# Row maxima of attention in the sampling taps: from single matmuls to pairs of heads

## What is computed

```
x = x + attention(gn(x))
    q, k, v = split(tokens @ w_qkv.T)
    attn = softmax(q @ k.T * SCALE) ; out = (attn @ v) @ w_proj.T + b_proj
x = x + gelu(batch_norm(deform_conv(gn(x))))
    offset = clip(conv(x, off_w)) ; mask = 2 * sigmoid(conv(x, mask_w))
    p = bilinear samples of x at tap + offset, times mask ; y = einsum(p, w)
```

## Time and profile before

| | |
|---|---|
| median of 3 runs | 3905.09 us (3904.13 to 3913.32) |
| profiled execution | 3908.9 us, its span 3907.0 us |
| mean granted TensorE clock | 0.959 of 2.4 GHz |
| TensorE busy | 3494.0 us (89%), 33434 matmuls |
| VectorE busy | 2220.8 us (57%) |
| ScalarE busy | 1628.7 us (42%) |
| GpSimd busy | 1216.0 us (31%) |

### The profile page before, as it was taken

How to read it: one execution, slowest core, us unless ns; L and a number is a source line. 1 busy time by engine, 2 the same in 40 slices (tenths; PEclk the granted TensorE clock), 3 DMA queues, 4 the chain that set the end, 5 groups by cost and what they waited for, 6 DMA issues and landing times.

```text
span 3907.0 us, 88793 instructions
## 1 busy us (share of the span) xinstructions
PE 3494.0 (89%) x33434; PEld 1884.3 (48%) x33434; DVE 2220.8 (57%) x3746; ACT 1628.7 (42%) x2644; POOL 1216.0 (31%) x1182
## 2 busy tenths in 40 slices
PE   5788999989999899898998899998999989998992
PEld 2244554545445454454544454454544545454661
DVE  5565565655655566555665556565565555655343
ACT  3054333633335434453335433363333633344443
POOL 0042232612325123332324233262232512333440
PEclk8689999999999999999998999999999999999896
DMA  3000000000000000000000000000000000001007
GB/s 125 1 18 34 1 1 35 3 33 1 1 35 2 33 1 2 36 34 1 1 2 36 34 1 1 23 15 33 1 1 35 2 33 1 1 19 66 1 1 291
DMA packets 12152, 97.81 MB, mean 25 GB/s; under 512 B 2777, under 2 KB 2905, under 8 KB 4972
## 3 DMA queue, kind: packets, MB, share of 16 engines
q1 hardware_dynamic: 9468, 67.41, 4.5%
q0 software_dynamic: 1152, 12.58, 0.8%
q10 hardware_dynamic: 1008, 11.01, 0.7%
HBM read 56.26 MB, written 34.60 MB: 23 GB/s over the span
## 4 chain that ended last, share of the span: by engine, by line
PE 53%; issue 24%; POOL 13%; ACT 4%; DVE 3%; DMA 1%; POOLq 0%; DVEq 0%; SPq 0%; ACTq 0%
PE R L1492 20%; PE R L1473 13%; POOL PL L607 12%; PE G L1270 7%; PE G L1237 5%; PE G L1461 2%; PE R L1385 2%; ACT PL L830 1%; PE G L1453 1%; PE R L1310 1%; PE G L1412 1%; ACT P L769 1%; PE G L1407 1%; DMA QK<-x_scratch 1%; DVE M L1166 0%
## 5 line engine op out<-in xcount | busy, mean ns | idle before, releaser
L1492 PE MATMUL R<-P,WALL 128*128 128x512 f16 x3888 | 984.8, 380 | 0.3 <-issue 0.3
L989 DVE TENSOR_REDUCE MXP<-G 128x1 f32<-128x512 f32 x1024 | 698.5, 689 | 257.6 <-PE G L1270 243.6
L607 POOL TENSOR_TENSOR PL<-P 128x1024 f16<-128x1024 f32 x256 | 515.7, 2017 | 760.2 <-ACT P L752 760.2
L1473 PE MATMUL R<-MHL,XB 128*128 128x240 f16 (+14 forms) x7776 | 726.3, 236 | 2.5 <-DVE P L1187 2.5
L644 POOL TENSOR_TENSOR MHL<-M,MHL 128x280 f16<-128x280 f32 (+2 forms) x576 | 364.6, 635 | 995.7 <-ACT MHL L840 994.5
L752 ACT ACTIVATE P<-R 128x1024 f32<-128x1024 f32 x512 | 521.0, 1023 | 306.1 <-PE R L1310 305.9
L1473 PEld LDWEIGHTS R<-MHL,XB 128*128 128x128 f16 x7776 | 536.3, 98 | 154.7 <-issue 108.6
L1492 PEld LDWEIGHTS R<-P,WALL 128*128 128x128 f16 x3888 | 345.3, 98 | 416.5 <-issue 95.6
L1039 DVE TENSOR_TENSOR PL<-P 128x1024 f16<-128x1024 f32 x256 | 366.0, 1430 | 292.0 <-ACT P L752 291.9
L1310 PE MATMUL R<-QK 48*128 48x512 f16 (+1 forms) x3072 | 444.0, 397 | 52.4 <-issue 32.3
L1270 PE MATMUL G<-QK 48*128 48x512 f16 x1024 | 412.6, 404 | 44.3 <-DVE QK L977 17.5
(11 more groups left out here) (125 smaller groups left out, 3235.1 us busy)
## 6 DMA issues: line engine op xcount, KB each, us to landing
XA<-x SPq DMA_DIRECT2D x8, 1536.0 KB, 8.9
X<-x SPq DMA_DIRECT2D x8, 1536.0 KB, 6.6
x_scratch<-X SPq DMA_DIRECT2D x7, 1536.0 KB, 5.1
y_scratch<-XP ACTq DMA_DIRECT2D x7, 1536.0 KB, 6.8
WALL<-y_scratch SPq DMA_DIRECT2D x6, 1536.0 KB, 15.1
out<-WALL POOLq DMA_DIRECT2D x6, 1536.0 KB, 10.9
QK<-x_scratch SPq DMA_DIRECT2D x4, 1536.0 KB, 17.6
P<-wd SPq DMA_DIRECT2D x9, 576.0 KB, 4.8
```

The lines of the kernel that those rows point to most:

```text
L607: pool.tensor_tensor(PL[:, s % P_BUFS, :], P32[:, s % P_BUFS, :], high_view(s), ALU.subtract).then_inc(p_low_pool, 1)
L989: dve.reduce_max(MXP[:, name[1] % 2, n // 2, n % 2:n % 2 + 1], chunk(sec, name)[:, :], AX.X).then_inc(dve_read, 1)
L1473: last = pe.matmul(out, XT[:, x_part, g * BOX_Y + r, t * 128:(t + 1) * 128], MHL[:, m_part, o + at:o + at + (hi - lo) * (x1 - x0)], start= ...
L1492: last = pe.matmul(R6[:, CT + ct, :], WALL[:, w:w + 128], PHL[:, u % 2, part // 2, t, :], start=(u % TAPS == 0 and n < CT), stop=(u % TAPS ...
```

## The change

The order of the maxima changes: for each tile and key half, head 0 and then head 1 (MAXIMA). In the samples they stand in columns 1 and 3, two in each, and none in 0 and 2. In the convolutions the second of a pair stands at the same spot as the first. Unit 0 has one pair, in column 3; units 1 to 5 have two pairs in the samples and one in the convolutions; units 6 to 17 two and two. `pos` stays at 2; `mask` stands where its place in the list puts it. The maxima before batch 0 keep their order (ALL_MAXIMA). Every matmul and every reduction is as it was, in form and number.

```
-MAXIMA = [("max", i, n) for i in range(PAIRS) for n in range(4 * QT)]
+MAXIMA = [("max", i, hd * 2 * QT + n) for i in range(PAIRS) for n in range(2 * QT) for hd in range(2)]
+ALL_MAXIMA = [("max", i, n) for i in range(PAIRS) for n in range(4 * QT)]
...
-    convs[0] = made[:3]
-    made = made[3:]
+    convs[0], made = made[:3], made[3:]
     due = []
-    for u in range(1, UNITS):
-        samples[u], maxima = maxima[:4], maxima[4:]
-        convs[u], due = due, []
-        convs[u] += made[:2]
-        made = made[2:]
-        count = 2 if u < 5 else 4
+    for u in range(UNITS):
+        first = 1 if u == 0 else 2
+        samples[u], maxima = [[]] * (4 - 2 * first) + sum(([[], maxima[2 * k:2 * k + 2]] for k in range(first)), []), \
+            maxima[2 * first:]
+        convs[u] += due
+        count = 0 if u == 0 else 2 if u < 6 else 4
+        convs[u] += made[:2] if u > 0 else []
+        made = made[2:] if u > 0 else made
         convs[u] += maxima[:count]
         maxima = maxima[count:]
...
-    return [("pos", u + 2)] + fills[:1] + [("mask", u + 2)] + fills[1:]
+    at = 2 if fills and fills[0][0] == "max" else 1
+    return [("pos", u + 2)] + fills[:at] + [("mask", u + 2)] + fills[at:]
...
-def spots(n):
-
-    return ([2, 6] + [13 + 13 * k // max(1, n - 2) for k in range(n - 2)])[:n]
+def spots(names):
+
+    out = []
+    for k, name in enumerate(names):
+        if name[0] == "max" and k and names[k - 1][0] == "max" and name[2] == names[k - 1][2] + 2 * QT:
+            out.append(out[-1])
+        elif name[0] == "pos":
+            out.append(2)
+        elif k == 1 and name[0] != "max":
+            out.append(6)
+        else:
+            out.append(13 + 13 * max(0, k - 1) // max(2, len(names) - 1))
+    return out
...
                             sample(u, c, 0, 0)
                             if not final and c < len(SAMPLE_FILL[u]):
-                                fill_chunk(SAMPLE_FILL[u][c], sec, b + 1)
+                                for name in SAMPLE_FILL[u][c]:
+                                    fill_chunk(name, sec, b + 1)
                             sample(u, c, 1, 0)
```

More of the change, by code:

```diff
@@ L128, in slot_fills @@
     samples, convs, maxima, made = [[] for _ in range(UNITS)], [[] for _ in range(UNITS)], list(MAXIMA), list(QK[5:])
-    convs[0] = made[:3]
-    made = made[3:]
+    convs[0], made = made[:3], made[3:]
     due = []
-    for u in range(1, UNITS):
-        samples[u], maxima = maxima[:4], maxima[4:]
-        convs[u], due = due, []
-        convs[u] += made[:2]
-        made = made[2:]
-        count = 2 if u < 5 else 4
+    for u in range(UNITS):
[6 more added lines that the diff above has]
+        made = made[2:] if u > 0 else made
         convs[u] += maxima[:count]
         maxima = maxima[count:]
-        due = [("maxT", n[1]) for n in samples[u] + convs[u] if n[0] == "max" and n[2] == 4 * QT - 1]
+        due = [("maxT", n[1]) for n in sum(samples[u], []) + convs[u] if n[0] == "max" and n[2] == 4 * QT - 1]
     if maxima or made or due != [("maxT", PAIRS - 1)]:
@@ L177, in start_chunks @@
         for k in range(4):
-            out += MAXIMA[(4 * i + k) * QT:(4 * i + k + 1) * QT]
+            out += ALL_MAXIMA[(4 * i + k) * QT:(4 * i + k + 1) * QT]
             if i + 1 < PAIRS:
@@ L205, in tap_chunks @@
             if start and c < len(SAMPLE_FILL[u]):
-                out += with_readers([SAMPLE_FILL[u][c]])
+                out += with_readers(SAMPLE_FILL[u][c])
             nu, nc = ahead(u, c, reach)
@@ L1178, in taps @@
                             if not final and c < len(SAMPLE_FILL[u]):
-                                read_chunk(SAMPLE_FILL[u][c], sec, b + 1)
+                                for name in SAMPLE_FILL[u][c]:
+                                    read_chunk(name, sec, b + 1)
                             nu, nc = ahead(u, c, reach)
@@ L1528, in taps @@
                         done = 0
-                        for name, end in zip(names, spots(len(names))):
+                        for name, end in zip(names, spots(names)):
                             if u > 0:
```

## The result

The changed kernel takes 3932.37 us (median of 6 runs, 3922.14 to 3941.38), the kernel before 3909.27 in the same comparison: a ratio of 1.0057, 95% interval 1.0038 to 1.0075. **It is slower by about 23 us**, where no change was forecast, with 3882 to 3930 as the range. The profiled execution took 3925.8 us against 3908.9.

What follows compares the result with a forecast made beforehand. TensorE was taken to set the pace of the taps, with VectorE mattering by when it gives a bank back. Unit gains and waits summed to 0.0 us a batch, times seven: no change, 3905 us, range 3882 to 3930.

Steps and rivals of the forecast that it cites:

- Unit 6 waits +0.9: Unit 5's mask moves from convolution 13 to 21, so unit 6 waits 0.9 us for the hats' halves.
- the prediction's sign: What would show the forecast right, here: unit 6 about 0.6 us longer than before.
- the ordinary unit: Units 7, 8, 9, 11, 12, 13, 15: samples +0.2, convolutions -0.4, so -0.2 us each, -1.2 a batch.
- B: A pair's second maximum, forecast to start 0.54 and 0.44 us after the first in sample columns 1 and 3.
- unit 12's own -0.5: Unit 12 no longer has an hy waiting for the maximum reduced behind the batch statistics: -0.5 us.
- The smaller terms (5, 10, 14, 16, 17): Unit 5 -1.1 us; units 10 and 14 -0.3 each; units 16 and 17 -0.5 in convolutions, -1.2 in samples.
- qk units: Units 1 to 4, with two projections and one pair in the convolutions: +0.9 us each, +3.6 in all.
- unit 0: Gains a pair it did not have, 0.43 us plus a bank wait of about 0.44: +0.9.
- The last batch makes no maxima and the start is untouched: Why the sum a batch, 0.0 us, was multiplied by seven and nothing else was counted.
- A: A pair's first maximum; in column 1 forecast to start 1.93 us into the unit, 0.05 after its bank's release.
- the third: Slower: B waits for its bank and holds TensorE's queue, or free-bank pairs do not overlap; 3918 to 3945 us, chance 0.24.
- Rival 2: Nearly the whole gain of 188 us, giving 3717 us, if banks were free when pairs are due; chance 0.02.

Runs made afterwards that it cites:

- the filler: The changed kernel plus five matmuls of 512 zero columns in unit 6 while TensorE would wait for the hats' half: 3946.43 us, ratio to before 1.0092.
- The run with columns 2 and 3: The changed kernel with the sample pairs of units 1 to 17 in columns 2 and 3 instead of 1 and 3: 3881.22 us, ratio to before 0.9936.
- with free banks: The changed kernel with pairs placed only where both banks have been read when their turn comes: 3788.42 us, ratio to before 0.9698.

## Why the prediction was wrong

**The step that failed first is unit 6's price.** "Unit 6 waits +0.9" had the mechanism, the place and nearly the size (0.95 idle, 1.1 in all), and no more: that TensorE's clock would fall behind this wait was not in the sum. It cost 1.3 us a batch, 9 us in seven, shown by the filler; the unit is 2.15 longer where the prediction's sign said about 0.6. The run with columns 2 and 3 shows that the wait alone doesn't bring the fall: with the pairs elsewhere the clock stayed at full behind the same 0.95 us. What else it needs stays open.

**The second is the ordinary unit**, forecast at -0.2 and measured at about 0. The sample stretch was right (+0.20). The convolutions gave 0.28 instead of 0.4: B of the first pair is 0.06 late, not free, since its bank is just being read (0.04 to 0.14 in the seven such units), and B behind the mask 0.51, not 0.41, because VectorE starts the mask's product 0.13 after the mask and not 0.04, the delay I had taken from a reduction behind its maximum. Of unit 12's own -0.5 little came: its samples fell from 7.24 to 7.18, where -0.3 was forecast with the pairs. With that the seven such units gave 1.2 us a batch less than forecast, 9 us in seven. The smaller terms (5, 10, 14, 16, 17) missed by 0.9 together, the two groups of qk units and unit 0 were within 0.3.

**The third is a thing that the sum took for fixed.** "The last batch makes no maxima and the start is untouched" is true, and the rest of each batch has no altered instruction either. But its time depends on the clock that it meets: 1349.8 us in the profile before, 1340.7 in the changed one, 1353 to 1371 in the nine others. In the changed kernel's profile that hid 9 of the 26 us of the taps (26.2 - 9.1 = 17.1 between the profiles, 16.9 measured); it was luck, and that one run, 3925.8 us, lies inside the forecast range. The changed kernel's six runs go from 3922.14 us at a mean granted clock of 0.961 to 3941.38 at 0.953. How that splits into taps and rest can't be read without their profiles, so the 23 us of the medians are the taps' 26 with a few us of something else around them. The median lies 2 us above the range; by these sums (an estimate) it would lie inside without the 9 us of the clock in unit 6, and also without the 9 us of the ordinary units.

**What was right:** what one maximum costs (0.42), that a pair costs as one; that B waits in the sample columns, by 0.54 and 0.44 (measured 0.55 and 0.46); that the saving of the samples is spent there; units 1 to 4 and unit 0. A matmul that waits for its bank starts 0.06 after the release, at the lower bound. The idle time before the maxima grew by 8 us a batch and not by some 20, because a B that is 0.55 late leaves the array idle only behind A's own 0.39. **Of the rivals, the third came true in its outcome** (slower, 3918 to 3945, its middle 3928) **but not by its mechanism**: pairs with free banks do overlap, and the 49 Bs of batch 0 that wait are 0.55 late in the mean, between my 0.5 and the 0.6 from which that rival would decide. Rival 2, that the whole gain would show, failed only by the places: with free banks 124.5 of the 188 us did come. The two rules of the Trainium skill weighed in the prediction (TensorE: Matmul & The Clock Gate, Part 3; TensorEngine Tiling, PSUM Bottleneck) both hold here: matmuls on distinct row groups run together (the pair at 22, two within 0.39 us), and the emptying of the banks decides (the same matmuls, placed otherwise, are 144 us apart).

## What to carry to other kernels

Before putting two chunks on end into two alternating banks, write down for each place who frees the second bank and when: the pair costs one only where both are free, and otherwise the second wait stands at the head of TensorE's queue. Here the same change was 0.6% slower in one table of places and 3.0% faster in another. An idle stretch of TensorE may cost more than itself, since the clock can fall behind it (1.3 us here for 0.95 idle, and nothing with the pairs in other columns), and parts of a program that no edit touches are to be measured apart, or a gain of 12 us in one part can vanish in another.

## What the runs showed of the hardware that was not expected

- 0.95 us of idle time of TensorE among short matmuls was followed by a stretch at half clock (granted clock 0.81 over 9.20 us) in every one of seven batches; the same time filled with matmuls on zeros was not, nor was the same idle time with the sample pairs in columns 2 and 3 (granted clock 1.00 over 7.40 us, seven of seven batches).
- The unchanged rest of a batch took 194.5 to 201.1 us in the six full periods of these profiles, longer where the granted clock was lower, and a constant delay of 1.73 us a batch elsewhere made the sum of seven 21 us longer.
- With both banks free, two 48-row matmuls of 512 columns on the same rows take 0.54 us from the first to the next convolution; two on different rows take 0.32, as a lone one does. Each has 0.10 more ahead for the switch of the array's form.
